# Two transformer layers on one core: causal masks as two half-height matmuls, setup inside the first token stage, first attention loads between the stores, layer 1 begins with its smallest block

## The reference, cut to what matters

```python
# x: (4, 1024, 128); T = 4096 tokens
xn = layernorm(x)
# layer 0: 16 heads of 8, a table of relative positions added to the scores
Q, K, V = proj(xn)
scores = (Q @ K.T + Q . rel_table[clip(i - j + 127, 0, 254)]) / sqrt(8)
s = softmax(scores) @ V @ Wo.T + bo
g = silu(one_of_8_experts(xn))            # argmax gate, one 128x128 matrix
x = x + s * g
xn = layernorm(x)
# layer 1: 8 differential heads (16 score maps of 8), causal
attn = softmax(q @ k.T + causal)          # causal: -inf above the diagonal
w = attn[:, :, 0] - lam * attn[:, :, 1]
s = rmsnorm_per_head(w @ v) * (1 - LAMBDA_INIT) @ Wo.T
g = silu(two_of_8_experts(xn))            # 128 -> 256 -> 128 with gelu
x = x + s * g
```

## Time and profile before

| | |
|---|---|
| median of 3 runs | 2192.43 us (2192.4 to 2195.33) |
| the profiled execution: time, span | 2193.76 us, 2190.9 us |
| PE busy | 1803.9 us (82%) |
| DVE, ACT, POOL busy | 1298.0, 1201.3, 1174.1 us |
| mean granted TensorE clock | 0.901 of full speed |
| HBM traffic | 61 GB/s over the span |

### The profile page before, as it was taken

One profiled execution on the slowest core, in us unless ns is written; L12 is line 12 of the kernel. 1 busy time (PEld: TensorE's weight loads), 2 busy tenths in 40 slices (PEclk: granted clock), 3 DMA queues, 4 the chain that ended last, 5 costly groups with the idle time before them and its releaser, 6 DMA issues. The chain is left out here.

```text
span 2190.9 us, 79090 instructions
## 1 busy us (share of the span) xinstructions
PE 1803.9 (82%) x33856; PEld 1340.6 (61%) x33856; DVE 1298.0 (59%) x1867; ACT 1201.3 (55%) x1441; POOL 1174.1 (54%) x1723
## 2 busy tenths in 40 slices
PE   3788079999898898898888859999958978878885
PEld 2666067777777776777777636666725545545553
DVE  4444067777577666776676424454467857657671
ACT  1332047777676777676767623444425645545563
POOL 4343168888587858777787621212004535445454
PEclk9888579999899999899999869999969989989997
DMA  1445412222321241221111121222321121211100
GB/s 54 138 121 144 137 50 61 64 64 81 85 62 58 63 103 55 64 64 56 52 53 57 50 78 58 61 70 66 97 63 25 28 60 32 49 31 28 28 23 14
DMA packets 166287, 139.57 MB, mean 64 GB/s; under 512 B 91713, under 2 KB 157138, under 8 KB 160450
## 3 DMA queue, kind: packets, MB, share of 16 engines
q1 hardware_dynamic: 145710, 100.76, 15.8%
q10 hardware_dynamic: 14868, 21.33, 3.9%
q0 software_dynamic: 5376, 12.59, 2.2%
HBM read 90.72 MB, written 43.12 MB: 61 GB/s over the span
## 5 line engine op out<-in xcount | busy, mean ns | idle before, releaser
L1304 ACT ACTIVATE a_EX<-bank 128x1024 f32<-128x1024 f32 x624 | 614.3, 1025 | 260.9 <-PE bank L1155 210.6
L1423 DVE TENSOR_TENSOR a_PM<-bank,a_PM 128x1024 f32<-128x1024 f32 x336 | 401.0, 1221 | 123.6 <-PE bank L1155 109.9
L1251 POOL TENSOR_TENSOR a_SN<-a_SN,a_MB 128x1024 f32<-128x1024 f32 x176 | 420.8, 2425 | 59.3 <-DMA a_MB<-m_dram 57.5
L1446 DVE TENSOR_REDUCE a_M<-bank 128x2 f32<-128x1024 f32 (+3 forms) x304 | 342.1, 1165 | 145.9 <-PE bank L1171 92.5
L1386 PE MATMUL bank<-a_EX,VV 128*32 128x128 f32 x9984 | 370.3, 293 | 1.9 <-issue 0.9
L1386 PEld LDWEIGHTS bank<-a_EX,VV 128*32 128x32 f32 x9984 | 277.9, 117 | 53.4 <-issue 26.9
L1155 PE MATMUL bank<-QS,KS 51*128 51x128 bf16 (+1 forms) x4992 | 238.0, 232 | 83.4 <-DMA QS<-a_MP 36.8
L1155 PEld LDWEIGHTS bank<-QS,KS 51*128 51x128 bf16 (+1 forms) x4992 | 159.5, 101 | 176.0 <-issue 48.7
L1300 ACT ACTIVATE a_SN<-bank 128x1024 f32<-128x1024 f32 x176 | 177.1, 1026 | 83.2 <-PE bank L1145 81.1
L1145 PE MATMUL bank<-QP,rel_t 112*128 112x32 bf16 x5632 | 198.3, 177 | 7.0 <-issue 6.7
L1308 ACT ACTIVATE a_SN<-a_SN 128x1024 f32<-128x1024 f32 x176 | 184.4, 1057 | 16.9 <-POOL a_SN L1251 16.4
(11 more groups left out here) (152 smaller groups left out, 2508.2 us busy)
## 6 DMA issues: line engine op xcount, KB each, us to landing
a_MB<-m_dram SPq DMA_DIRECT2D x32, 1024.0 KB, 5.0
QS<-q_dram SPq DMA_DIRECT2D x176, 96.0 KB, 3.0
KS<-k_dram ACTq DMA_DIRECT2D x14, 768.0 KB
q_dram<-t_PARTS SPq DMA_DIRECT2D x32, 192.0 KB, 2.8
k_dram<-t_PARTS SPq DMA_DIRECT2D x16, 384.0 KB, 2.9
QS<-a_MP SPq DMA_DIRECT2D x384, 2.0 KB
KR<-kr_dram ACTq DMA_DIRECT2D x8, 576.0 KB
q_dram<-t_PARTS SPq DMA_DIRECT2D x32, 128.0 KB, 2.4
```

The lines of the kernel that those rows point to most:

```text
L1251: pool.tensor_tensor(near_view(sn), near_view(sn), as_near(MB[:, :, :], it.part), ALU.add)\
L1304: act.activation(as_banks(EX[:, it.need % ER[layer]], part), by_head, ACT.Exp, scale=SCALE).then_inc(act_done, 1)
L1423: dve.tensor_tensor(pm, mb.rearrange("p hh (k i) -> p hh k i", k=4), pm, ALU.max).then_inc(max_used, 1)
L1446: dve.tensor_reduce(target.rearrange("p (hh k) -> p hh k", hh=2)[:, :, p0:p0 + g], mb[:, :, 0:g * width].rearrange("p hh (k j) -> p hh k j ...
```

## The change

Causal masks go in row tiles: `mask_b` holds the identity and both masks split in two halves of 64 rows, and each half is added on its own half of the array. The setup block is dissolved: 7 loads (`first_loads`) go ahead of everything on SP, 9 (`late_loads`) behind the weights of the experts; POOL fills the buffers after its work for groups 0 to 3; DVE makes the tables in the expert steps 1, 3, 5 and 7 of group 0; `lam_s` is finished after the last group. PE waits for `first_in` alone, ACT for `bias_ready`. In both layers, SP issues `load_kv(0)` behind the stores of group 4, `load_q(0)` and `load_q(1)` behind those of group 5, `load_q(2)` and `load_q(3)` behind those of group 6. Layer 1 takes its blocks as 0, 7, 1, 6, 2, 5, 3, 4. The planner's costs, switches, due times and windows have other values, for both layers, so that the written-out order of both attention stages is another one.

```diff
     k = u % NB
-    return k if layer == 0 else (NB - 1 - k // 2 if k % 2 == 0 else k // 2)
+    return k if layer == 0 else (k // 2 if k % 2 == 0 else NB - 1 - k // 2)
...
-COST = {"far": 270, "near": 1290, "maxt": 880, "mstore": 400, "mb": 700, "av": 870, "mrow": 110, "oback": 440, "oturn": 110, "oproj": 430,
-        "mask": 450, "evict": 1028, "nexp": 1068, "ocopy": 600, "oturned": 277, "mcopy": 277,
-        "take": 1221, "nmax": 1225, "nlast": 1350, "split": 1300, "onorm": (613, 1056), "final": 300, "add": 1600,
-        "nsub": 2480, "perm": 6480, "orms": 8540, "rows": 4000, "seen": 310, "told": 80, "rows_in": 2100, "mb_in": 5700, "q_in": 3000, "kv": 3300}
+COST = {"far": 270, "near": 1290, "maxt": 880, "mstore": 400, "mb": 700, "av": 930, "mrow": 110, "oback": 440, "oturn": 110, "oproj": 430,
+        "mask": 480, "evict": 1028, "nexp": 1068, "ocopy": 600, "oturned": 277, "mcopy": 277,
+        "take": 1221, "nmax": 1600, "nlast": 1900, "split": 1300, "onorm": (613, 1056), "final": 300, "add": 1000,
+        "nsub": 2560, "perm": 6480, "orms": 9000, "rows": 4000, "seen": 310, "told": 80, "rows_in": 2100, "mb_in": 5700, "q_in": 3000, "kv": 3300}
 SHAPE = {"max": "rows", "exp": "rows", "av": "columns"}
-SWITCH = {"rows": {"columns": 115, "all": 120}, "columns": {"rows": 175, "all": 180}, "all": {"rows": 90, "columns": 90}}
+SWITCH = {"rows": {"columns": 135, "all": 130}, "columns": {"rows": 200, "all": 185}, "all": {"rows": 90, "columns": 90}}
...
-    {"max": (-0.98, 0.76), "mrow": (-1.19, 1.31), "msplit": (-1.8, -3.97), "exp": (1.16, 0.54),
-     "av": (6.26, -0.28), "out": (2.38, -0.04)}]
-NEAR_BY, STAY = (247, 250), (0.77, 1.47)
+    {"max": (-0.81, 0.85), "mrow": (-0.48, -1.07), "msplit": (-0.68, -5.27), "exp": (1.42, 0.55),
+     "av": (4.94, -0.81), "out": (1.65, 1.53)}]
+NEAR_BY, STAY = (178, 207), (0.27, 0.85)
...
+                    def fill(f):
+
+                        if f == 0:
+                            pool.memset(QN[:, :, :, :, :, :].bitcast(F32), 0.0)
+                            pool.memset(QP[:, :, :, :, :].bitcast(F32), 0.0)
+                            pool.memset(ones_row[:, :], 1.0)
+                        elif f < 3:
+                            pool.memset(KS[:, f - 1, :, :].bitcast(F32), TWO_ONES)
+                            pool.memset(KR[:, f - 1, :, :].bitcast(F32), TWO_ONES)
+                        else:
+                            pool.memset(VV[:, :, :, :], 0.0)
+                        pool.drain()
+                        if f == 3:
+                            pool.sem_inc(setup_done, 1)
+
...
-                    with pool.Fori(0, GROUPS - 2) as f:
+                    for f in range(4):
+                        load_x(f + 2)
+                        parts(f)
+                        scale(f + 2)
+                        if layer == 0:
+                            fill(f)
+                    with pool.Fori(4, GROUPS - 2) as f:
                         load_x(f + 2)
                         parts(f)
                         scale(f + 2)
...
-                    sp.wait_ge(qk_stored, QKS * 2 + 1)
-                    sp.wait_ge(v_stored, 32 + 1)
-                    if layer == 1:
-                        load_q(layer, sp, 0)
-                        load_q(layer, sp, 1)
-                        load_kv(layer, sp, 0)
+                    for f in range(2, GROUPS):
+                        store_v(f)
+                        store_gate(f - 2)
+                        store_qk(f // 2, f % 2)
+                        if f == 4:
+                            if layer == 0:
+                                sp.wait_ge(setup_done, 1)
+                            sp.wait_ge(qk_stored, QKS * 2 + 1)
+                            sp.wait_ge(v_stored, 32 + 1)
+                            load_kv(layer, sp, 0)
+                        elif f > 4 and f < GROUPS - 1:
+                            for u in range(2 * (f - 5), 2 * (f - 4)):
+                                load_q(layer, sp, u)
                     store_gate(GROUPS - 2)
                     store_gate(GROUPS - 1)
...
+                    def first_biases():
+                        dve.wait_ge(first_in, 16 * len(first_loads))
+                        dve.tensor_scalar(bk2[:, 0:1], col[:, 1:2], col[:, 2:3], None, ALU.add)
+                        dve.tensor_scalar(bk2[:, 1:2], col[:, 1:2], col[:, 3:4], None, ALU.add).then_inc(bias_ready, 1)
+                        dve.tensor_copy(pick_e[:, :, :], eye[0:E, 0:E, None].broadcast_to([E, E, P]))
+                        dve.drain()
...
                     def body(kind, f, p, k):
+                        if kind == "expert" and layer == 0 and k % 2 == 1 and type(f) is int and f == 0:
+                            attention_tables(k)
...
+            def mask_rows(pe, it, which):
+
+                for part in range(2):
+                    for hh in range(2):
+                        rows = slice(hh * HALF, (hh + 1) * HALF)
+                        last = pe.matmul(bank[:, 2 * it.n + hh, :].rearrange("p (h c) -> p h c", h=4), mask_b[rows, 0, part, :],
+                                         mask_b[rows, which, part, None, :].broadcast_to([HALF, 4, P]), start=False,
+                                         stop=part == 1, skip_group_check=True)
+                return last
...
                 if masked:
-                    for hh in range(2):
-                        last = pe.matmul(bank[:, 2 * it.n + hh, :].rearrange("p (h i) -> p h i", h=4), eye_b[:, :],
-                                         mask_b[:, 1:2, :].broadcast_to([P, 4, P]), start=False, stop=True,
-                                         skip_group_check=True)
+                    last = mask_rows(pe, it, 2)
...
                 def _(sp):
-                    if layer == 1:
-                        for u in range(2, QR):
-                            load_q(layer, sp, u)
                     for it in plan["sp"]:
```

More of the change, by code:

```diff
@@ L167, in attention_tasks @@
                 columns = 2 * step.part[2] * step.part[4]
-                cost = columns * 0.258 + (COST["mask"] + SWITCH["rows"]["all"] if step.jb == ib else 0)
+                cost = columns * 0.258 + (COST["mask"] if step.jb == ib else 0)
                 taken.append(ring(step, cost, "dve", columns * 1.035 + 160, loaded, i / len(m), [(last("mrow", u - 2), seen)])[1])
@@ L195, in attention_tasks @@
                 for c in range(2):
-                    cost = COST["far"] + (COST["mask"] + SWITCH["rows"]["all"] if layer == 1 and jb == ib else 0)
+                    cost = COST["far"] + (COST["mask"] if layer == 1 and jb == ib else 0)
                     made, exps[jb, c] = ring(Step("exp", u, jb, c), cost, "act", COST["evict"], rows + [(last("exp", 0), 0)],
@@ L268, in attention_plan @@
             shape = wanted
-            if layer == 1 and it.jb == block_order(1, it.u) and it.kind in ("max", "exp"):
-                shape = "all"
             if it.kind in ("max", "maxt", "near", "exp"):
@@ L388, in build @@
         eye = sb("eye", [P, P])
[L389 to L390 removed]
+        mask_b = sb("mask_b", [P, 3, 2, P], BF16)
         rank = sb("rank", [P, GT, E])
@@ L804, in _ @@
                     run(act, body)
+                    if layer == 0:
+                        act.wait_ge(lam_sum, 1)
+                        act.activation(lam_s[:, 0:2], lam_s[:, 0:2], ACT.Exp).then_inc(lam_exp, 1)
                 @block.tensor
@@ L1174, in row_scores @@
                 if seg == 0:
-                    for hh in range(2):
-                        last = pe.matmul(bank[:, 2 * it.n + hh, :].rearrange("p (h j) -> p h j", h=4), eye_b[:, :],
-                                         mask_b[:, 0:1, :].broadcast_to([P, 4, P]), start=False, stop=True,
-                                         skip_group_check=True)
+                    last = mask_rows(pe, it, 1)
                 return last
```

144 lines of the change are left out of this document (59 added, 85 removed).

## The result

The changed kernel took **2126.82 us** (median of 4 runs, 2120.13 to 2131.26) against 2192.41 (4 runs) for the kernel before on the same chip: ratio 0.9705, 95% interval 0.9662 to 0.9748. Run again beside the first experiments it gave 2126.29 us, ratio 0.9731 (0.9679 to 0.9783). The forecast of 2129 us is 2 us off, and the range of 2088 to 2157 holds. As will be seen, the sum came out by luck: two errors cancel.

The account below looks back on a forecast made before the run. PE was taken to set the pace, loosely, in both attention stages. Terms -17.0 - 32.0 + 5 - 4.5 - 2 - 14 + 1 = -63.5 gave 2129 us, 2.9% below; range for 8 in 10: 2088 to 2157.

Parts of the forecast that it names:

- Setup: Head of the kernel: POOL's load of `X` issued earlier, so PE starts earlier, -17.0 us; added fills and tables taken as 0.
- First loads of layer 0: End of layer 0's token stage: without ACT's 12 loads of `QS` the stage ends near 224.7 instead of 256.7, -32.0 us.
- +5, the middle and a little over, since it is one queue: Layer 0's token stage: moved loads on SP delay group 5's stores by 5 us, between 0 (engines share) and 9.
- the middle loads are not hidden: Rival, layer 0's token stage: 33 us of loads all land on the store loop, border gives nothing, 2157 us; chance 0.10.
- the rule that I weighed: Layer 0's token stage: moved loads stand wholly ahead of the next stores, delay the full 9 us, boundary worth 23, not 27.
- First loads of layer 1: End of layer 1's token stage: last gate's store no longer behind loads, -4.5 us; wait for unit 2's queries gone, -2.
- Masks: Layer 1's attention stage: 0.22 us saved in each of 128 masked slots, 28 us of PE time, half taken: -14 us.
- the masks are free already: Rival, layer 1's attention stage: POOL's chain sets the pace, saved PE time turns into waits, 2143 us; chance 0.12.
- The new order: Both attention stages: the planner's new values move prices both ways, so the new order of steps was taken as 0.
- The rival that put a gain here: Both attention stages: the new order closes a fifth of PE's idle 232 us, 46 us, giving 2083 us; chance 0.17.
- The rival that put a loss here: Attention stages: lower `STAY` makes PE change shape more often, 0.11 us each; at twelve more per unit 2213 us; chance 0.03.
- Block order: Layer 1's attention stage: smallest block first, maxima of block 7 later, two more exponentials on the tail: +1, between -3 and +4.

Follow-up runs that it names:

- the first experiments: The first three follow-up runs, beside which the changed kernel was run again; the kernel before had a median of 2188.38 us (16 runs) there.

## Why the prediction was right, and where it was not

**Setup: right.** PE's first matmul moved by 17.1 us, forecast 17.0, and the fills are hidden as worked out. Group 5's `PARTS` came at 137.88, where 153.54 - 17.1 = 136.4 would be due, so fills and tables cost 1.4 us at most: inside the 0 to 5 that I gave them. That moment lies between 133.6 and 137.9 in the eight profiles with this token stage, so the 1.4 may be nothing. The Trainium skill's rule ("SBUF — State Buffer", "SBUF: two separate sides"), by which DVE and POOL lock one another out of a shared port, would have allowed more; that 1.4 is all that any blocking of DVE by the fills can have cost. With the loads at their old place the stage is 20.9 us shorter, 3.8 more than the head shows: ACT's held issue is 36.53 instead of 37.93 us, which is 1.4 of it, and it starts 19.4 us earlier instead of 17.1. Of before itself one profile has this stage 5.2 us shorter than the other (252.1), so the 3.8 needs no cause.

**First loads of layer 0: right mechanism, one term mis-sized.** "Without these loads on ACT the last gate goes right behind PE's last matmul" held to 0.04 us, and "about 3 us" for its store was 3.4. The step that failed is the price ahead of it: "+5, the middle and a little over, since it is one queue", between 0 and 9. The first issue was forecast at 213 and came at 225.17, so by the sum's own terms the price was 17 us. Against the kernel with the loads at the end it is 19.9: PE's last matmul ends at 221.70 instead of 201.81. Of these, 1.2 are there at group 5, 14.7 lie in the step between the two `PARTS` (39.4 - 24.7) and 4.0 behind it; of the last, 1.6 are PE's final 32 matmuls, 5.48 us for 3.84, at a granted clock of 0.68 and 1.00. The gain from there to the first issue is 30.6 us for the forecast 32.

The length of the transfer was right: from 136.29 to the end of the held store at 161.66 are 25.4 us, at 134 GB/s, as the forecast had it (25 us from 136.4 on). Counted from 152.4, when the stores were due, that is 9.3, the upper bound. What failed is the middle: I took it that the engines would share, and the stores waited for all of it. Beyond the bound came 2.9 for the issue of a gate store that stood behind the held one, and 1.9 because the q and k stores were slower (12.7 us from the first issue to `PARTS`, 10.75 before), with the 190 GB/s of 162 to 190 beside them. `X` of a later group was late too. A bound made of one delayed transfer was no bound. The rival "the middle loads are not hidden" had 33 us for this price, and over half of it came true.

After that it was open whether size or queue was to blame. Pieces for each gap took 14.0 us off the stage, and the two `PARTS` were 26.1 us apart; on another queue they were 39.9 apart, no less than on SP's. So the rule that I weighed, that descriptors of one ring are taken in order while rows of rings alternate (the Trainium skill, "DMA: Bandwidth & Descriptors", "Queues, rings and completion order"), had the size of the price more nearly than my 5, but not its cause: with the loads on the other row the step was as long. The cause that is left is the transfer's size in one gap. That nothing else is in the 14.0 is not shown, as the pieces also start earlier.

**First loads of layer 1: right.** 5.1 us for 4.5, and the last gate's wait for its store is gone. The wait for unit 2's queries is gone too; its 2 us can't be seen in the stage, which is as long with the wait back (580.4).

**Masks: right for one slot, wrong for PE's sum and for the path.** A slot costs 0.66 us as forecast (0.65). But PE's busy time in the stage fell by 11.3 us under the old order and 9.9 under the new, not by the 28 of 128 such slots. The slots with a full-height turn behind them, where nothing is gained, are some 6 us of the difference; the rest is open. Of "between 0 and -28" I took half. It was 7 us under the old order and nothing visible under the new one. This was my rival "the masks are free already": with the new order it is the case that came true, though not by POOL's chain alone: against the run with the old masks the waits for `OF` are 31.4 us for 26.6 and those for rows of maxima 33.1 for 30.4. The 14 us that stage 2 of layer 1 did lose come from block order and planner values together (6 to 7 us, under the new masks) and from the masks under the old order (7 us), and in whichever order one takes the parts away the shares differ; they can't be added up part by part.

**The new order: the step that failed.** "I take 0." The planner's values were worth 21 us in layer 0's attention stage (1019.3 to 998.4) and, with the new block order and without the rule for masks, 23 us in layer 1's. By the bound that I set myself, 15 us beyond the masks, the prediction of this part was wrong. The argument looked at single values (`orms` up, `add` down, `STAY` lower) as if each had a sign of its own, and the runs with half of them show that it hasn't: alone, either half loses over 20 us in layer 0. The rival that put a gain here (a fifth of the idle time, by shorter waits) had the right side and the wrong source: PE's idle time fell by 4 us in layer 0 and not at all in layer 1. In layer 0 16 of 20 us are busy time (10 to 16, as the same order had PE busy for 864.8 to 870.4 us in seven profiles). The rival that put a loss here counted shape changes. In the two written-out orders they go from 711 to 717 in layer 0: six more, not nine in each unit. In layer 1 they go from 528 to 467, but 42 of the 61 fewer are the masks themselves, which no longer leave PE at full height. Which of the values makes the order better isn't shown. As the work is the same, what is left is how the steps of the engines meet; that is argued, not measured.

**Block order: +1 with the new values was wrong by itself.** With the old values it costs 17 us, with the new ones it gives 18 to 19. Counting slots at the head and exponentials on the tail missed what the rows of waits show: the block order moves 25 us of waiting onto the rows of maxima and takes some off the turn of `OF`, and how much it takes off depends on the values.

**The sum.** Loads of layer 0 gave 16 us less than forecast and the setup 4 more, the order of layer 0's attention stage 20 more, and the rest agrees to within 2: -63.5 forecast, -70.3 in the profiles, -65.6 between the medians.

## What to carry to other kernels

A transfer hidden between others has to fit its gap as a whole, with everything that is issued behind it counted, loads for later groups too; if it does not, cut it and spread the pieces over more gaps before trying another queue, which did nothing here. Removing work from an engine that idles a fifth of a stage is worth what the order of steps leaves of it, so measure it under the order that it will run with. Fitted values of a planner are one edit: no value's sign can be read by itself, and an unrun order deserves a wide range around zero, here 2% (all values) to 4% (half of them) of the attention stage's time, and not a bare zero. Before a few us are put down to a cause, look how far profiles of the same code differ in that stage, here by up to 12.5 us.

## What the runs showed of the hardware

- An engine's queue can be held for tens of us in the issuing of a DMA that is itself small: 21.62 us for one store of `V` by SP behind five issues of keys and values, 0.36 with the same data in pieces; 11.24 us for three issues in the run with the keys on ACT's queue. So the other queue does not free the issuing engine.
- POOL's copy behind a drain, with its own four small loads ahead, started after 10.27 us of idle while keys were loading, and after 0.47 us when they were not. The profile marks both as idle for "issue" and names no releaser. The slowest load of `a_XG` took 13.4 us to land, and the last of the four was issued at 227.39: the sum, 240.8, is near the copy's 241.10. Before, 258.92 and 13.9 make 272.8, for a copy at 272.73. So the drain may wait for these loads; no run tests it.
- The mean granted clock of layer 0's attention stage went with the length of the stage, from 0.90 at 1040.1 us to 0.93 at 998.4, and the same 22848 matmuls took 887 to 865 us.
- Two full-height mask matmuls and eight half-height scores matmuls took 0.86 us at full clock, four half-height masks and the same scores 0.66; with a full-height turn behind the masks the two ways cost the same.
